# Attention 0 of a fused two-layer decoder: another order of ScalarE's and VectorE's work within a slot

## The reference

```python
q = (layernorm(x) @ wq).reshape(b, 64, 32, 128)      # 32 query heads of 128
k = (ctx @ wk).reshape(b, 64, 8, 128)                # 8 key/value heads, each for 4 query heads
v = (ctx @ wv).reshape(b, 64, 8, 128)
scores = einsum('bqhd,bkhd->bhqk', q / sqrt(128), k)
out = einsum('bhqk,bkhd->bqhd', softmax(scores), v).reshape(b, 64, 4096)
x = x + out @ wo
```

## Time and profile before

| | |
|---|---|
| median of 3 runs | 1640.8 us (1638.39 to 1643.19) |
| profiled execution, its own time | 1641.23 us |
| span of that execution in the trace | 1639.5 us |
| mean granted TensorE clock | 0.973 of full speed |
| TensorE matmul, busy | 1485.9 us (91%) |
| VectorE, busy | 1267.8 us (77%) |
| ScalarE, busy | 858.3 us (52%) |
| GpSimd, busy | 305.9 us (19%) |

### The profile page before, as it was taken

How to read it: one execution, slowest core, us unless ns; L and a number is a source line. 1 busy time by engine, 2 the same in 40 slices (tenths; PEclk the granted TensorE clock), 3 DMA queues, 4 the chain that set the end, 5 groups by cost and what they waited for, 6 DMA issues and landing times. The chain is left out here.

```text
span 1639.5 us, 29417 instructions
## 1 busy us (share of the span) xinstructions
PE 1485.9 (91%) x11227; PEld 780.1 (48%) x11227; DVE 1267.8 (77%) x2276; ACT 858.3 (52%) x1776; POOL 305.9 (19%) x271
## 2 busy tenths in 40 slices
PE   6999999999999999999999887799999987777695
PEld 4455455455545554555555443344444444443253
DVE  4877876777677677777777786899888886999777
ACT  3554552343424434434334332688888854888552
POOL 0032130011111102010111100011111103789620
PEclk9999999999999999999999998899999999999898
DMA  6287573214231231414132223122232340876402
GB/s 243 83 173 164 128 169 85 78 52 104 58 97 51 64 102 35 130 27 115 51 102 64 52 103 117 24 45 46 45 62 50 59 97 5 154 110 110 76 1 103
DMA packets 317143, 140.73 MB, mean 86 GB/s; under 512 B 265856, under 2 KB 290560, under 8 KB 316800
## 3 DMA queue, kind: packets, MB, share of 16 engines
q1 hardware_dynamic: 273936, 98.14, 28.3%
q10 hardware_dynamic: 43120, 41.42, 8.3%
HBM read 66.13 MB, written 11.53 MB: 47 GB/s over the span
## 5 line engine op out<-in xcount | busy, mean ns | idle before, releaser
L638 PE MATMUL xp<-WO,OT 128*128 128x512 f16 x1536 | 340.4, 382 | 4.1 <-DVE X L925 4.1
L599 PE MATMUL pj<-XT,WQ 128*128 128x512 f16 x1536 | 338.9, 380 | 5.5 <-DVE WQ L284 4.9
L638 PEld LDWEIGHTS xp<-WO,OT 128*128 128x128 f16 x1536 | 148.3, 98 | 187.3 <-issue 16.2
L599 PEld LDWEIGHTS pj<-XT,WQ 128*128 128x128 f16 x1536 | 148.1, 98 | 181.6 <-issue 7.1
L756 ACT ACTIVATE E<-E 128x512 f32<-128x512 f32 x64 | 40.2, 628 | 300.8 <-DVE E L902 300.8
L1163 PE MATMUL db<-W0T,XD 128*128 128x448 f16 x768 | 156.7, 363 | 15.9 <-DVE XD L1361 11.0
L925 DVE SCALAR_TENSOR_TENSOR X<-xp,X 128x512 f32<-128x512 f32 x128 | 88.2, 689 | 91.1 <-PE xp L638 90.1
L1181 PE MATMUL eb<-W1T,DT 128*128 128x512 f16 x672 | 149.2, 382 | 4.2 <-ACT eb L1268 4.2
L573 POOL TENSOR_TENSOR VW<-VW,XB 128x1024 f32<-128x1024 f32 x14 | 33.0, 2356 | 615.0 <-DVE VW L102 615.0
L862 DVE SCALAR_TENSOR_TENSOR QT<-pj,QT 128x512 f16<-128x512 f32 x128 | 87.9, 687 | 70.8 <-ACT QT L726 70.8
L1163 PEld LDWEIGHTS db<-W0T,XD 128*128 128x128 f16 x768 | 75.7, 100 | 94.6 <-DVE XD L1361 12.0
(11 more groups left out here) (239 smaller groups left out, 2465.7 us busy)
## 6 DMA issues: line engine op xcount, KB each, us to landing
W0T<-in_L_xattn_wo ACTq DMA_DIRECT2D x15, 1024.0 KB, 5.5
W0T<-in_L_xattn_wq SPq DMA_DIRECT2D x9, 1024.0 KB, 5.5
W0T<-in_L_xattn_wq ACTq DMA_DIRECT2D x7, 1024.0 KB, 5.6
X<-in_x SPq DMA_DIRECT2D x4, 1024.0 KB, 7.6
out<-X SPq DMA_DIRECT2D x8, 512.0 KB, 3.6
XB<-in_L_ffn_W ACTq DMA_DIRECT2D x28, 128.0 KB, 3.0
w0t<-XB ACTq DMA_DIRECT2D x7, 512.0 KB, 7.4
w1t<-W0T ACTq DMA_DIRECT2D x7, 512.0 KB, 7.9
```

What stands on the lines that cost most here:

```text
L599: last = pe.matmul(bank[:, :], w, src[:, b, k, tokens], start=n == 0, stop=n == 3 * KC - 1)
L638: last = pe.matmul(xp[i % 2][:, :], OT[:, a, j, i * P:(i + 1) * P], WO[:, b, j, :], start=n == 0, stop=n == 3 * REP - 1)
```

## The change

The order of ScalarE's and VectorE's work behind `probabilities` is changed in each slot. TensorE's, SP's and GpSimd's programs stay as they are, and no instruction is added or removed.

- ScalarE takes the high halves of units 2 and 3 directly behind `probabilities`, and `high_o` after them.
- ScalarE takes outputs 0 ahead of unit 4 (keys) and not behind it. `weights_times_rec` and `load_weights` move from ahead of unit 4 to behind it; in the first slots `high_inputs(.., 0)` comes behind `high_o` and `high_inputs(.., 1)` behind unit 4.
- VectorE takes unit 3 ahead of `low_o`, and outputs 0 ahead of unit 4. In the last group `x_ahead(0)` and `first_x[1]` come behind unit 3, and `x_ahead(1)` behind unit 4.
- `high_weights` and `low_weights` stay ahead of unit 4, and are now directly ahead of outputs 0.
- Two semaphores, of the sums and of their reciprocals, become one, with counts to match.

```diff
             def first_slot(cur, nxt):        # ScalarE
                 ahead = 1 <= cur.n <= AHEAD_SLOTS
                 probabilities(cur, nxt)
+                high(nxt, (2, 3))
                 high_o(cur)
-                high(nxt, (2,))
                 if ahead:
                     high_inputs(cur.n - 1, 0)
-                high(nxt, (3,))
+                high_out(cur, 0)
+                high(nxt, (4,))
                 if ahead:
                     high_inputs(cur.n - 1, 1)
-                high(nxt, (4,))
-                high_out(cur, 0)
                 high(nxt, (5,))
                 high_out(cur, 1)
...
             def later_slot(g, t, nxt, first, last):        # ScalarE
                 probabilities(cur, nxt)
+                if nxt:
+                    high(nxt, (2, 3))
                 if t == 1:
                     high_o(cur)
-                if nxt:
-                    high(nxt, (2, 3))
-                if t > 1 and not last:
-                    weights_times_rec(g, *PIECES[t - 2])
-                if last and t in (1, 2):
-                    stats_x(act, t - 1)
                 if t == 1 and not first:
                     high_weights(g - 1, *PIECES[1])
                 if t == 3 and not last:
                     high_weights(g, *PIECES[0])
+                if last and t in (1, 2):
+                    stats_x(act, t - 1)
+                high_out(cur, 0)
+                if nxt:
+                    high(nxt, (4,))
+                if t > 1 and not last:
+                    weights_times_rec(g, *PIECES[t - 2])
                 if t == 1 and not last:
                     ...
                     load_weights(act, g)
-                if nxt:
-                    high(nxt, (4,))
-                high_out(cur, 0)
                 if nxt:
                     high(nxt, (5,))
                 high_out(cur, 1)
...
             def first_slot(cur, nxt):        # VectorE
                 probabilities(cur, nxt)
+                low(nxt, 3)
                 low_o(cur)
-                low(nxt, 3)
+                low_out(cur, 0)
                 low(nxt, 4)
-                low_out(cur, 0)
                 low(nxt, 5)
                 low_out(cur, 1)
...
             def sums(cur, jp):        # VectorE
-                at = count(cur, 2, jp + 1)
-                dve.wait_ge(S["exp_done"], at)
-                dve.reduce_sum(ST[:, 1, jp, :], E[:, jp, :, :], AX.X).then_inc(S["sum_done"], 1)
-                dve.wait_ge(S["sum_done"], at)
-                dve.reciprocal(ST[:, 2, jp, :], ST[:, 1, jp, :]).then_inc(S["rcp_done"], 1)
+                dve.wait_ge(S["exp_done"], count(cur, 2, jp + 1))
+                dve.reduce_sum(ST[:, 1, jp, :], E[:, jp, :, :], AX.X).then_inc(S["sum_step"], 1)
+                dve.wait_ge(S["sum_step"], count(cur, 4, 2 * jp + 1))
+                dve.reciprocal(ST[:, 2, jp, :], ST[:, 1, jp, :]).then_inc(S["sum_step"], 1)
...
                 probabilities(cur, nxt)        # VectorE, later_slot
+                low(nxt, 3)
                 if t == 1:
                     low_o(cur)
                 x_ahead(0)
                 if last and t == 2:
                     first_x[1](dve)
-                low(nxt, 3)
-                x_ahead(1)
                 if t == 1 and not first:
                     low_weights(g - 1, *PIECES[1])
                 if t == 3 and not last:
                     low_weights(g, *PIECES[0])
+                low_out(cur, 0)
                 low(nxt, 4)
+                x_ahead(1)
                 x_ahead(2)
-                low_out(cur, 0)
                 low(nxt, 5)
                 low_out(cur, 1)
                 x_ahead(3)
```

More of the change, by code:

```diff
@@ L429, in attention0 @@
         names = ("o_hi o_lo sc_done pj_done pt_done pv_done xp_done "
-                 "exp_done pj_hi e_hi ot_hi max_done sub_done sum_done rcp_done p_done pj_lo e_lo ot_lo x_acc "
+                 "exp_done pj_hi e_hi ot_hi max_done sub_done sum_step p_done pj_lo e_lo ot_lo x_acc "
                  "wb_ld wb2_ld wa_done wstep ww_done wcut wbits wm_done wsum wqs_done wq_done wt_done wt_hi wt_lo w_st "
@@ L905, in sums @@
             def sums(cur, jp):
-                at = count(cur, 2, jp + 1)
-                dve.wait_ge(S["exp_done"], at)
-                dve.reduce_sum(ST[:, 1, jp, :], E[:, jp, :, :], AX.X).then_inc(S["sum_done"], 1)
-                dve.wait_ge(S["sum_done"], at)
-                dve.reciprocal(ST[:, 2, jp, :], ST[:, 1, jp, :]).then_inc(S["rcp_done"], 1)
+                dve.wait_ge(S["exp_done"], count(cur, 2, jp + 1))
+                dve.reduce_sum(ST[:, 1, jp, :], E[:, jp, :, :], AX.X).then_inc(S["sum_step"], 1)
+                dve.wait_ge(S["sum_step"], count(cur, 4, 2 * jp + 1))
+                dve.reciprocal(ST[:, 2, jp, :], ST[:, 1, jp, :]).then_inc(S["sum_step"], 1)
             def normalise(cur, jp):
-                dve.wait_ge(S["rcp_done"], count(cur, 2, jp + 1))
+                dve.wait_ge(S["sum_step"], count(cur, 4, 2 * jp + 2))
                 dve.tensor_tensor(E[:, jp, :, :], E[:, jp, :, :], ST[:, 2, jp, :].unsqueeze(2).to_broadcast([P, BB, SEQ]),
```

## The result

| | median | lowest to highest | ratio to before, 95% interval |
|---|---|---|---|
| before, in the same series | 1639.72 us | 1638.39 to 1643.19 (4 runs) | |
| changed | 1622.01 us | 1621.99 to 1622.19 (4 runs) | 0.9885 [0.9871, 0.9900] |

The change gains 1.1%, 17.7 us by the medians; 1622.01 us lies inside the forecast's own range of 1616 to 1624, 2.2 us above the 1619.8 that it names. The profiled execution went from 1641.23 to 1622.19 us and its span from 1639.5 to 1620.5: 19.0 less, where 21.0 was forecast.

What follows compares the result with a forecast made beforehand. TensorE's matmuls were taken to bound attention 0 (96% of first slots, 98% of loop). Slot and last-group gains total 21.5 us, less 0.5 for PT: 21.0, so 1641.2 becomes 1620.2 profiled, 1619.8 median; range 1616 to 1624.

Steps and rivals of the forecast that it cites:

- Unit 4's wait gone, unit 5's too: Attention 0 slots before the last group: TensorE's stalls of 0.76 to 1.65 us at unit 4 and 0.25 at unit 5 vanish.
- Outputs 0 just in time in the slots with `low_o`, 1.04 late in the loop's t = 1: VectorE ends outputs 0 0.1 us before the second product in nine slots; loop's t = 1 swaps 1.42 for 1.04, gaining 2.28.
- the moved wait, the rival at 1631: Slots with `low_o`: hand-overs 0.5 us later keep about 0.5 of each stall in 16 slots, plus PT waits; chance 0.10.
- t = 3: Seven t = 3 slots: the second product's wait for outputs 0 vanishes, 0.94 us each, 6.58 in all.
- `low_o` ahead of GpSimd: Slots n = 1 to 6: `low_o` starts before GpSimd's first difference and takes 2.28 us, not 3.27.
- the rival at 1625: GpSimd still holds `low_o` in n = 1 to 6 (3.27 us), so 5.4 us less gain; chance 0.10.
- PT: Probabilities' DMAs landing late for the first product in attention 0's slots: 0.5 us off in all, bounds 0 and 3.
- Last group: Last group of attention 0, bound by VectorE in t = 1: gain 0.8 us for t = 1 and t = 2 together.
- t = 2 gains 0.4: Last group's t = 2: second product at 967.0 us, not 969.74; less VectorE idling and GpSimd lock-out gain 0.4.
- the rival at 1665: Attention 0 slots: without pauses TensorE is granted about 0.95 clock, losing 45 us; chance 0.05, shared with any other loss.

Runs made afterwards that it cites:

- the first half alone: Kernel before with units 2 and 3 ahead of `high_o` and unit 3 ahead of `low_o`, outputs 0 left behind unit 4: 1643.06 us, ratio 1.0004.
- the kernel with the extra instruction: Changed kernel plus an unused VectorE maximum (0.68 us) directly ahead of outputs 0: 1629.63 us with its tile behind all other buffers, 1631.23 with it ahead of EH and PT.
- the second half alone: Changed kernel with `high_o` and `low_o` back in their old places, outputs 0 still ahead of unit 4: 1631.16 us, ratio 0.9924.
- the shifted tiles: Changed kernel with 32 or 64 unused bytes ahead of EH and PT: 1625.23, 1623.08 us; with 0.68 us more VectorE work ahead of outputs 0 or `low_o`: 1631.23, 1625.04.
- the last two kernels of this question: Changed kernel, t = 1 weight halves behind unit 4, last group's t = 1 `x_ahead` spread: 1612.76 us; then `x_ahead(0)` ahead of unit 3 in t = 1 and 2: 1609.32.

## Why the prediction was right, step by step

- **Unit 4's wait gone, unit 5's too.** Shown: none in the trace, and the first half alone takes them all away. The even n, n = 7 and the first t = 1 came to 0.02 us of their forecast.
- **Outputs 0 just in time in the slots with `low_o`, 1.04 late in the loop's t = 1.** Shown: the second product starts at T+17.67, 0.03 off. Without `low_weights` in the queue that wait is gone, and with 0.68 us more in it 0.5 to 0.6 comes back in each slot with a `low_o`. So the moved wait, the rival at 1631, was some 0.6 us away in nine slots, and the kernel with the extra instruction comes near its 1631 (1629.6).
- **t = 3.** 0.94 each forecast and measured; it comes from the second half alone.
- **`low_o` ahead of GpSimd.** Shown in both traces: in the changed kernel all 16 `low_o` take 2.29 us. In n = 2 of the changed kernel VectorE starts first and keeps its time, and GpSimd's first difference is the long one; before, it was the other way round:

```profile
113.25 2.29 DVE L874 SCALAR_TENSOR_TENSOR WO<-W0T,WO 128x2048 f16<-128x2048 f32 x1 [1.11 <-ACT WO L740]
```

```profile
113.82 2.75 POOL L567 TENSOR_TENSOR XB<-XB 128x512 f16<-128x512 f32 x1 [22.23 <-ACT XB L751]
```

  GpSimd's 2.75 less 1.16 is 1.59, near the 1.72 that VectorE still had to run. The order of issue decides who pays, and the rival at 1625 fell. By the rule of the Trainium skill ("SBUF — State Buffer", section "Who interferes with whom") the first to issue keeps the port for its whole instruction; the trace agrees, with 2.29 us for VectorE when it is first and 3.27 when it is second.
- **PT: more than forecast.** Forecast 0.5, measured 0.9 (0.62 in n = 1, 0.29 more in t = 2 of group 1), within its bounds of 0 and 3. That is not a difference one trace can settle: the wait in t = 2 of group 1 came out at 0.39 and at 1.18 us in two traces with the order of before. The mechanism was right: with the stall ahead of it gone, the first product has 0.2 us of room and a late landing shows. The traces of the shifted tiles show what it costs if the landing is 0.4 later.
- **Last group: its t = 2 read wrongly.** Forecast 0.8, measured 0.0. VectorE does start the first `accumulate` of t = 1 at T+28.17 (28.04 forecast, 28.35 before), and t = 1 and t = 2 take 35.57 and 20.14 us for 35.80 and 23.50. But the last slot takes 40.21 us and not 36.66. The second product itself came where it was forecast, at T+20.53 in t = 1 and T+17.98 in t = 2. In the changed kernel's trace:

```profile
915.19 0.83 PE L627 MATMUL tv<-PT,V 64*128 64x256 f16 x12 [3.87 <-DVE OT L870]
915.95 7.04 PE L638 MATMUL xp<-WO,OT 128*128 128x512 f16 x24
923.66 5.34 PE L638 MATMUL xp<-WO,OT 128*128 128x512 f16 x24 [0.67 <-DVE X L923]
...
961.29 6.77 PE L638 MATMUL xp<-WO,OT 128*128 128x512 f16 x24 [5.57 <-DVE X L923]
```

  The step "t = 2 gains 0.4" looked at the second product and not at the output tiles of t = 2 behind the last scores, of which the third now waits 5.57 us for VectorE's `accumulate` (1.77 before). VectorE's work in the whole stretch is the same (79.6 us busy in 96.1, 80.1 in 96.2 before), and an earlier product shortened none of it. Spreading that work did: up to the next part's bias matmul, the last two kernels of this question take 96.6 and 93.6 us for the changed kernel's 101.4.
- **The start.** The first scores come 0.7 later, a term that the prediction didn't have. The traces show where they arise: the first 48 matmuls of the projections start at 21.10 us in both, behind an idle time of 4.90 us, and take 11.98 us before and 12.70 in the changed kernel, at a mean granted clock of 0.87 and 0.82 (windows 21.10:32.90 and 21.10:33.60). The edit does not touch them, and over all kernels run they took 11.80 to 13.42 us and the first scores started between 37.99 and 39.56, with no pattern that follows the edits. So this term is the clock of that stretch, which differs from trace to trace.

```profile
21.10 11.98 PE L599 MATMUL pj<-XT,WQ 128*128 128x512 f16 x48 [4.90 <-DVE WQ L284]
...
21.10 12.70 PE L599 MATMUL pj<-XT,WQ 128*128 128x512 f16 x48 [4.90 <-DVE WQ L284]
```

  The first line is of before, the second of the changed kernel. Without this term and the 0.4 gained behind the last group, the part that was forecast came to 19.3 against 21.0.
- **The clock.** The rival at 1665 fell: the slots are granted 1.00 with 99% of the time filled.

## What to carry to other kernels

When a stall is taken from a matmul that waits for a queue of another engine, lay out that queue to its end, since the stall stands up again at the next matmul that it feeds unless that one is moved too. Here the first half gained 2.9 us in the slots, the second 6.1, and both 19.3. Ahead of a tight hand-over, put work into time in which the engine waits anyway (0.68 us ahead of `low_o` left the loop's t = 1 at 30.20 us, and behind it made it 0.6 longer). And where engine and matmuls are both full, the last group of a stage is worth an order of its own: it gave 7.8 us, two fifths of what the change gave.

## What the runs showed of the hardware

- **The address of the transposing DMAs' tiles.** The DMAs that write PT from EH land in 2.8 us (median of 64), and in 3.2 us with both tiles, and those behind them, 32 or 64 bytes further on in each partition. The median is 2.8 in all nine kernels with the tiles in place, with 1 to 3 waits for PT in the slots, and 3.2 in all four with the shift, with 7 to 17 waits. 32 bytes of unused memory lengthened the slots by 3.6 us, in one trace. The cause is open.
- **TensorE after a pause.** The windows of the changed kernel in the last group: ahead of the 3.87 us pause, in it, two stretches behind it, and the run behind the next gap of 0.67 us (columns of the earlier trace rows).

```profile
893.26:911.00 17.74, 17.74 (x167) 10.18 (x166) 14.69 (x21) 8.62 (x11) 4.25 (x2) 1.00 0.20 46
911.30:915.19 3.89, 0.02 (x3) 0.01 (x2) 3.85 (x11) 2.15 (x5) 0.00 (x0) 1.00 0.01 1
915.20:918.50 3.30, 3.30 (x20) 1.41 (x21) 3.09 (x11) 1.09 (x2) 0.00 (x0) 0.69 0.53 133
918.50:923.00 4.50, 4.49 (x18) 1.74 (x16) 4.50 (x9) 0.00 (x0) 0.00 (x0) 0.85 0.56 194
923.66:929.00 5.34, 5.34 (x30) 2.50 (x31) 2.79 (x12) 2.56 (x5) 0.00 (x0) 1.00 0.00 0
```

  The granted clock is 1.00 up to the pause and falls behind it, to means of 0.69 and 0.85 between the levels of 2.4 and 1.2 GHz. 24 matmuls took 7.04 us there and 5.34 behind the short gap, so behind a pause of 3.87 us 1.7 more were lost. The gaps of 1.0 us in the loop cost nothing beside themselves: with one, a slot takes 30.20 us and not 29.12.
